# V of an attention kernel turned in blocks on VectorE instead of on TensorE and ScalarE

## Chip, core and metric

The kernel runs on one core of one Trainium2 chip. Times are device microseconds (us) of that core, from the first to the last instruction of an execution.

## What is computed

Eight sequences of 256 tokens (2048 tokens in all), model width 512. Layer norm, then causal attention with 32 query heads and 8 key/value heads of 128, rotary embedding, and scores of some keys scaled; beside it a gate network of four low-rank experts with a top-2 router. Cut to the attention and the end:

```
xn = layernorm(x)
q, k, v = xn @ wq.T, xn @ wk.T, xn @ wv.T        # heads of 128
q, k = q*cos + rotate_half(q)*sin, k*cos + rotate_half(k)*sin
scores = q @ k.T / sqrt(128) * key_scale + causal
attn = softmax(scores) @ v
out = x + (attn @ wo.T) * silu(gate_network(xn))
```

All is fp32. A product of two fp32 matrices is made of three passes on TensorE: each operand is split into a high part (fp32r, written by ScalarE: k_high, q_high, v_high, rows_high, attn_high) and a low part (the difference, by VectorE: k_low, q_low, v_low, rows_low, attn_low), and high x high, high x low and low x high are added in PSUM.

## The kernel before

**Units.** The work is cut into 32 units: 8 key/value heads by 4 blocks of 512 tokens (two sequences). A unit u has four items j of two query heads and one sequence each, n4[1] to n4[4]. Every engine has its own instruction list, written out by hand in one order: pe_unit (L629), act_unit (L936), dve_unit (L1322), and group for GpSimd (L422). Engines are tied by semaphores alone. Units 8 to 30 run in a loop, the others are unrolled; the opening, unit 0 and the closing have lists of their own (act_opening L1007, dve_opening L1399). In units 0 to 7 pieces of the gate network (pe_side, act_side, dve_side) stand between the steps.

**TensorE in unit u**, in order: turn_probs(0), output tile (1,0) of the unit before, scores(2), prob_value(0), output tile (1,1); turn_probs(1), projection of H1 for unit u+1, scores(3), prob_value(1), projection of H2, projection of V (L510 into bank_a); turn_probs(2), projection of H3, scores(0) of unit u+1, prob_value(2), projection of K for unit u+2 into bank_a (it waits for vT_done, L695), projection of H0 for u+2; turn_probs(3), output tile (0,0), scores(1) of u+1, prob_value(3), turn_v, output tile (0,1). H0 to H3 are the four query heads that share the unit's K and V. A projection is 12 matmuls of 512 columns (three_pass), an output tile too.

**V's way.** V is projected as the other kinds are, with its 128 dimensions on the partitions and the 512 tokens along them. prob_value needs it with the tokens on the partitions. So copy_vT on ScalarE (L879) moves the bank to v_T in SBUF, which also frees bank_a for K; later turn_v on TensorE (L567, four transposes of 128x128) writes it back turned into bank_a, once K's rotation has read that bank; v_high (L886) and v_low (L1264) split it from the bank into v_hi and v_lo, and prob_value(0) of the next unit waits for v_ready.

**A query head's way.** Projection, swap_halves on ScalarE (L857, L858, which move the partition halves crosswise into rot), sin_product on GpSimd (L399) beside cos_product on VectorE (L1240), rotate on VectorE (L1249, the sum of both), q_high (L865), q_low (L1255). next_scores on TensorE (L611) waits for pT_ready, that is rows_low of the item that used the same pair of banks, and for q_ready, that is q_low and k_low: scores(0) for K, H0 and H1, scores(1) for H2 and H3.

**An item's way.** scores, low_scores on ScalarE (L892), mask_rows on VectorE (L1286 to L1295), exponents (L907), row_inverse (L1305), normalise_rows (L918), turn_probs (L588), rows_high (L926) and rows_low (L1275), prob_value (L597), attn_high (L933) and attn_low (L1270), output tiles (L604), which add_tile on VectorE (L1315) adds to y_sum.

**GpSimd** also splits the weights of the next key/value head (split, L382 and L385), at fixed places of every group of four units.

## Time and profile before

| | us |
|---|---|
| median of 3 runs | 1327.3 |
| lowest and highest | 1326.88, 1327.61 |
| the profiled execution | 1326.8 |
| its span in the trace | 1324.6 |

Busy in the span: TensorE 98%, VectorE 72%, ScalarE 73%, GpSimd 32%; the granted TensorE clock is 0.999 of full. The chain that ended last lies on TensorE for 92% of the span. A timeline row gives the start, the length and the instruction; where the next row of the same engine starts before the end of this one, the two overlapped, so the distance of two starts (the step) is what an instruction costs in a row of them. The ends of matmuls are modelled.

### The profile page before, as it was taken

The numbers are of one execution on the slowest core, as the hardware profiler recorded it, in microseconds if no ns is written. First come the engines' busy times: TensorE is split into PE (matmuls) and PEld (weight loads), VectorE is DVE, ScalarE is ACT, GpSimd is POOL, SyncE is SP. The second block draws the span as 40 slices with busy tenths as digits, with TensorE's granted clock in tenths as the row PEclk, the third lists the DMA queues.
The fourth block names the chain that finished last, engine by engine and source line by source line (L and its number), as shares of the span: only waits on it lengthen the run. The fifth ranks groups of instructions, "written<-read, shape, count | busy, mean of one in ns | idle before, by whom it ended". The sixth has DMA issues, their size and how long they took to land.

```text
span 1324.6 us, 22633 instructions
## 1 busy us (share of the span) xinstructions
PE 1303.3 (98%) x7000; PEld 1106.3 (84%) x7000; DVE 953.7 (72%) x2438; ACT 972.5 (73%) x2529; POOL 427.0 (32%) x345
## 2 busy tenths in 40 slices
PE   8899999999999999999999999999999999999998
PEld 7688788888888888888888888888888888888876
DVE  7776678777777677777767777767777767777776
ACT  6877577877778777778777777777677877776874
POOL 5413312423214332233414124141431433224323
PEclk9999999999999999999999999999999999999999
DMA  6000000201101000000100001010000101002124
GB/s 230 24 1 21 25 8 9 65 28 53 40 17 32 15 25 8 16 16 16 27 5 24 8 16 32 0 32 0 24 24 0 32 8 32 8 20 95 52 82 150
DMA packets 23530, 43.66 MB, mean 33 GB/s; under 512 B 2496, under 2 KB 2752, under 8 KB 23488
## 3 DMA queue, kind: packets, MB, share of 16 engines
q1 hardware_dynamic: 20896, 38.74, 9.5%
q10 hardware_dynamic: 2592, 4.40, 0.9%
q8 instruction: 21, 0.34, 0.1%
q14 instruction: 21, 0.17, 0.0%
HBM read 34.74 MB, written 8.39 MB: 33 GB/s over the span
## 4 chain that ended last, share of the span: by engine, by line
PE 92%; ACT 3%; DVE 3%; issue 1%; DMA 0%; DVEq 0%; ACTq 0%
PE bank_b L510 19%; PE bank_a L510 18%; PE bank_b L604 13%; PE o_ps L604 12%; PE pv_ps L597 10%; PE pair L581 8%; PE pair L588 6%; PE pair L577 2%; PE pair L579 1%; PE o_ps L510 1%; PE bank_a L567 1%; ACT x_sb L1000 1%; ACT probs L918 0%; ACT probs L907 0%; ACT rot L857 0%
## 5 line engine op out<-in xcount | busy, mean ns | idle before, releaser
L399 POOL TENSOR_TENSOR rot<-rot,tab 128x512 f32<-128x512 f32 x160 | 207.1, 1296 | 593.2 <-ACT rot L858 592.9
L907 ACT ACTIVATE probs<-probs,row_min 128x128 f32<-128x128 f32 (+1 forms) x512 | 225.7, 447 | 0.2
L926 ACT ACTIVATE pT_hi<-pair 128x768 fp32r<-128x768 f32 x128 | 104.0, 812 | 164.5 <-PE pair L588 163.7
L918 ACT ACTIVATE probs<-probs,row_inv 128x128 f32<-128x128 f32 (+1 forms) x512 | 190.6, 445 | 22.5 <-DVE row_inv L1305 22.1
L1275 DVE TENSOR_TENSOR pT_lo<-pair,pT_hi 128x768 fp32r<-128x768 f32 x128 | 121.6, 950 | 86.1 <-ACT pT_hi L926 85.9
L382 POOL TENSOR_TENSOR w_hi<-raw,zero 128x512 fp32r<-128x512 f32 x74 | 85.0, 1148 | 243.4 <-PE bank_a L510 126.5
L510 PE MATMUL bank_a<-xT_hi,w_hi 128*128 (+1 forms) x376 | 149.9, 399 | 0.2 <-DVE xT_lo L1145 0.2
L510 PE MATMUL bank_b<-xT_hi,w_hi 128*128 (+1 forms) x376 | 149.8, 398 | 0.0
L510 PE MATMUL bank_b<-xT_hi,w_lo 128*128 (+1 forms) x376 | 146.8, 390 | 0.0
L510 PE MATMUL bank_a<-xT_hi,w_lo 128*128 (+1 forms) x376 | 146.8, 390 | 0.0
L510 PE MATMUL bank_a<-xT_lo,w_hi 128*128 (+1 forms) x376 | 146.3, 389 | 0.0
L510 PE MATMUL bank_b<-xT_lo,w_hi 128*128 (+1 forms) x376 | 146.3, 389 | 0.0
L1255 DVE TENSOR_TENSOR q_lo<-cosx,q_hi 128x512 fp32r<-128x512 f32 x128 | 117.2, 917 | 36.0 <-ACT q_hi L865 35.8
L581 PE MATMUL pair<-k_parts,q_hi 128*128 128x256 f32 x512 | 116.7, 309 | 0.0
L588 PEld LDWEIGHTS pair<-tab,probs 128*128 128x128 f32 x768 | 90.9, 139 | 22.7 <-ACT probs L918 6.8
L588 PE MATMUL pair<-tab,probs 128*128 128x128 f32 x768 | 104.8, 272 | 4.6 <-ACT probs L918 4.6
L1286 DVE CUSTOM_DVE_ANT_0 probs<-pair,tab 128x256 f32<-128x256 f32 x256 | 106.4, 416 | 0.0
L604 PE MATMUL o_ps<-w_hi,attn_hi 128*128 128x512 f32 x252 | 104.2, 413 | 0.3 <-DVE attn_lo L1270 0.3
L1240 DVE TENSOR_TENSOR cosx<-bank_b,tab 128x512 f32<-128x512 f32 x94 | 64.7, 689 | 52.6 <-ACT rot L858 52.0
L604 PE MATMUL bank_b<-w_hi,attn_hi 128*128 128x512 f32 x252 | 101.6, 403 | 0.0
L385 POOL TENSOR_TENSOR w_lo<-raw,w_hi 128x512 fp32r<-128x512 f32 x74 | 99.5, 1345 | 5.8
L604 PE MATMUL bank_b<-w_hi,attn_lo 128*128 128x512 f32 x252 | 98.9, 393 | 0.0
(181 smaller groups left out, 3277.3 us busy)
## 6 DMA issues: line engine op xcount, KB each, us to landing
raw<-w_seq SPq DMA_DIRECT2D x76, 256.0 KB, 2.6
gate_scratch<-b_raw ACTq DMA_DIRECT2D x16, 256.0 KB, 2.0
out<-y_sum SPq DMA_DIRECT2D x16, 256.0 KB, 2.0
x_sb<-x SPq DMA_DIRECT2D x3, 1024.0 KB, 11.2
mid<-x SPq DMA_DIRECT2D x7, 256.0 KB, 2.8
mid<-gate_scratch SPq DMA_DIRECT2D x7, 256.0 KB, 3.5
raw<-x SPq DMA_DIRECT2D x7, 256.0 KB, 2.7
raw<-gate_scratch SPq DMA_DIRECT2D x7, 256.0 KB, 2.9
```

The lines of the kernel that those rows point to most:

```text
L399: nc.gpsimd.tensor_tensor(v, v, tab[:, s:s + SEQ].unsqueeze(1).to_broadcast([P, 2, SEQ]), ALU.mult).then_inc(sin_done[kind], 1)
L510: mm = nc.tensor.matmul(dst, w(a, c), xs[:, c, bass.ds(x0, BLOCK)], start=(c == 0 and n == 0), stop=(c == DC - 1 and n == 2))
L581: mm = nc.tensor.matmul(ps[:, h, 2 * P:], a[:, head, late], k[:, k1], start=(n == 0), stop=(n == 2))
L588: mm = nc.tensor.transpose(ps[:, h, s * P:(s + 1) * P], probs[:, j % 2, h, s * P:(s + 1) * P], ident)
L597: mm = nc.tensor.matmul(dst, v[:, 2 * b + kb, :], p[:, :, c:c + (P if kb else SEQ)], start=(i == 0), stop=(i == 5))
L604: mm = nc.tensor.matmul(bank, a[:, h, rows], w[:, WO + h, :], start=(h == 0 and i == 0), stop=(h == GROUP - 1 and i == 2))
L907: a = nc.scalar.activation(s, s, ACT.Exp, bias=row_min[:, j % 2, i:i + 1], scale=-1.0, accum_out=row_sum[:, i:i + 1])
L918: a = nc.scalar.activation(s, s, ACT.Copy, scale=row_inv[:, i:i + 1])
L926: nc.scalar.activation(pT_hi[:, :, :], pair[j % 2][:, :, 0:ROWS], ACT.Copy).then_inc(pThi_done, 1)
L1255: nc.vector.tensor_tensor(q_lo[:, h, :], cosx[:, BUF[kind], :], q_hi[:, h, :].bitcast(F32), ALU.subtract)\
L1275: nc.vector.tensor_tensor(pT_lo[:, :, :], pair[j % 2][:, :, 0:ROWS], pT_hi[:, :, :].bitcast(F32), ALU.subtract).then_inc(pT_ready, 1)
L1286: return nc.vector.tensor_tensor_reduce(out=probs[:, par, h, s], in0=(probs[:, par, h, 0:P], pair[par][:, h, 2 * P:])[qt], in1=tab[:, T_MA ...
```

## The change

V's bank is turned straight into v_T. turn_v_blocks on VectorE issues eight transposes for each half: each takes 32 partitions of bank_a (32 of V's dimensions) by 4 x 32 columns (32 tokens of each of the four tiles), turns its four 32x32 blocks, and writes 32 partitions by 4 x 32 columns of v_T. Inside a half the read partitions change with every instruction, the written ones after every fourth. copy_vT and turn_v go (but for the first V, which keeps both); v_high and v_low read v_T. The K projection that follows V in bank_a waits for both halves (vturn_done) instead of the copy. The lists of ScalarE and VectorE, in the units and in the opening, are put into another order. TensorE's order is the same but for turn_v.

The opening's lists are left out below; in them the same steps stand in another order, and the transposes of the second V stand before q_low(H1) and after it.

```diff
@@ -353,7 +354,7 @@
             sp.wait_ge(q_ready[H2], UNITS)
             load_xg(TILES - 1, 2)
             sp.wait_ge(q_ready[K], UNITS)
-            sp.wait_ge(vt_ps, UNITS)
+            sp.wait_ge(v_ready, UNITS)
             load_xg(TILES - 2, 3)
             for s in range(2):
                 store_tile(TILES - 6 + s)
@@ -562,7 +563,7 @@
             three_pass(bank[:, :], lambda w, c: (w_hi, w_lo)[w][:, chunk, c * P:(c + 1) * P], x0)\
                 .then_inc(proj_done[kind], 1)
 
-        def turn_v(bank=bank_a):
+        def turn_v(bank):
             for t in range(BLOCK_TILES):
                 mm = nc.tensor.transpose(bank[:, t * P:(t + 1) * P], v_T[:, t * P:(t + 1) * P], ident)
             mm.then_inc(vt_ps, 1)
@@ -692,7 +693,7 @@
             if ahead:
                 if isinstance(u, int) and u < BLOCKS - 2:
                     pe.wait_ge(xlo_done, BLOCK_TILES * (u + 3))
-                pe.wait_ge(vT_done, c2)
+                pe.wait_ge(vturn_done, value(pe, 2 * u + 2))
                 project(K, bank_a, WK, x_2, w_2)
             pe_side(u, 2, 2)
             if ahead:
@@ -709,12 +710,6 @@
             pe.wait_ge(pT_ready, n4[4])
             pe.wait_ge(attn_ready, n4[3])
             prob_value(3)
-            if not last:
-                if ahead:
-                    bank_free(K, c3)
-                else:
-                    pe.wait_ge(vT_done, c2)
-                turn_v()
             if not last:
                 bank_free(*((H0, c3) if ahead else (H3, c2)))
             output_tile(0, 1, n4[2], n4[0] if last else None)
@@ -871,19 +866,20 @@
                 act.wait_ge(scores_done, used)
             nc.scalar.activation(k_hi, k_full[:, :], ACT.Copy).then_inc(qhi_done[K], 1)
 
-        def copy_vT(count, before_count, bank=bank_a):
+        def copy_first_vT():
+            nc.scalar.wait_ge(proj_done[V], 1)
+            nc.scalar.activation(v_T[:, :], FIRST_V, ACT.Copy).then_inc(vT_done, 1)
+
+        def first_v_high():
+            nc.scalar.wait_ge(vt_ps, 1)
+            nc.scalar.activation(v_hi[:, :, :], pv_ps[:, :].rearrange("p (k d) -> p k d", k=BLOCK_TILES),
+                                 ACT.Copy).then_inc(vhi_done, 1)
+
+        def v_high(turned, used):
             act = nc.scalar
-            act.wait_ge(proj_done[V], count)
-            if before_count is not None:
-                act.wait_ge(vt_ps, before_count)
-            nc.scalar.activation(v_T[:, :], bank[:, :], ACT.Copy).then_inc(vT_done, 1)
-
-        def v_high(count, used, bank=bank_a):
-            act = nc.scalar
-            act.wait_ge(vt_ps, count)
-            if used is not None:
-                act.wait_ge(pv_done, used)
-            nc.scalar.activation(v_hi[:, :, :], bank[:, :].rearrange("p (k d) -> p k d", k=BLOCK_TILES),
+            act.wait_ge(vturn_done, value(act, 2 * turned))
+            act.wait_ge(pv_done, used)
+            nc.scalar.activation(v_hi[:, :, :], v_T[:, :].rearrange("p (k d) -> p k d", k=BLOCK_TILES),
                                  ACT.Copy).then_inc(vhi_done, 1)
 
         def low_scores(j, done):
@@ -941,56 +937,56 @@
             rows_high(0, n4[1], None if first else n4[0])
             normalise_rows(1, n4[2])
             low_scores(2, n4[3])
+            attn_high(0, n4[1], None if first else n4[-2])
             if not last:
                 q_high(H0, c2, n4[3])
+            exponents(2, n4[3])
             rows_high(1, n4[2], n4[1])
-            attn_high(0, n4[1], None if first else n4[-2])
-            exponents(2, n4[3])
             act_side(u, 1, 0)
             if not last:
                 swap_halves(H1, bank_a, c2, H0, c2)
             low_scores(3, n4[4])
+            if not last:
+                k_high(c2, n4[4])
             act_side(u, 1, 1)
-            if not last:
-                k_high(c2, n4[4])
             normalise_rows(2, n4[3])
+            if not last:
+                swap_halves(H2, bank_b, c2, K, c2)
             attn_high(1, n4[2], None if first else n4[-2])
-            if not last:
-                swap_halves(H2, bank_b, c2, K, c2)
             act_side(u, 1, 2)
             if not last:
                 q_high(H1, c2, n4[3])
             act_side(u, 1, 3)
             rows_high(2, n4[3], n4[2])
             exponents(3, n4[4])
+            if not last:
+                swap_halves(H3, bank_b, c2, H1, c2)
             act_side(u, 2, 0)
             if not last:
-                copy_vT(c2, c1)
-                swap_halves(H3, bank_b, c2, H1, c2)
                 low_scores(0, n4[5])
+            normalise_rows(3, n4[4])
             act_side(u, 2, 1)
-            normalise_rows(3, n4[4])
+            attn_high(2, n4[3], None if first else n4[0])
             if not last:
                 q_high(H2, c2, n4[4])
-            attn_high(2, n4[3], None if first else n4[0])
             act_side(u, 2, 2)
+            if is_unit(u, 1):
+                b_high()
             if ahead:
                 swap_halves(K, bank_a, c3, H2, c2)
-            if is_unit(u, 1):
-                b_high()
             if not last:
                 q_high(H3, c2, n4[4])
             if ahead:
                 swap_halves(H0, bank_b, c3, H3, c2)
+            rows_high(3, n4[4], n4[3])
             act_side(u, 2, 3)
-            rows_high(3, n4[4], n4[3])
             if not last:
                 exponents(0, n4[5])
                 low_scores(1, n4[6])
                 normalise_rows(0, n4[5])
             attn_high(3, n4[4], None if first else n4[0])
             if not last:
-                v_high(c2, n4[4])
+                v_high(c1, n4[4])
                 exponents(1, n4[6])
 
         def x_shifted(t0, t1, count):
...
@@ -1259,9 +1254,28 @@
             nc.vector.wait_ge(qhi_done[K], count)
             nc.vector.tensor_tensor(k_lo, k_full[:, :], k_hi.bitcast(F32), ALU.subtract).then_inc(q_ready[K], 1)
 
-        def v_low(count, bank=bank_a):
+        def turn_v_blocks(count, half):
+
+
+            dve = nc.vector
+            dve.wait_ge(proj_done[V], count)
+            dve.wait_ge(v_ready, value(dve, count - 1))
+            src = bank_a[:, :].rearrange("p (t i a) -> p t i a", t=BLOCK_TILES, i=4)
+            dst = v_T[:, :].rearrange("p (t d) -> p t d", t=BLOCK_TILES)
+            for i in range(2 * half, 2 * half + 2):
+                for j in range(4):
+                    ins = nc.vector.transpose(dst[32 * i:32 * i + 32, :, 32 * j:32 * j + 32],
+                                              src[32 * j:32 * j + 32, :, i, :])
+            ins.then_inc(vturn_done, 1)
+
+        def first_v_low():
+            nc.vector.wait_ge(vhi_done, 1)
+            nc.vector.tensor_tensor(v_lo[:, :, :], pv_ps[:, :].rearrange("p (k d) -> p k d", k=BLOCK_TILES),
+                                    v_hi[:, :, :].bitcast(F32), ALU.subtract).then_inc(v_ready, 1)
+
+        def v_low(count):
             nc.vector.wait_ge(vhi_done, count)
-            nc.vector.tensor_tensor(v_lo[:, :, :], bank[:, :].rearrange("p (k d) -> p k d", k=BLOCK_TILES),
+            nc.vector.tensor_tensor(v_lo[:, :, :], v_T[:, :].rearrange("p (k d) -> p k d", k=BLOCK_TILES),
                                     v_hi[:, :, :].bitcast(F32), ALU.subtract).then_inc(v_ready, 1)
 
         def attn_low(j, done):
@@ -1337,153 +1351,160 @@
             mask_rows(2, n4[3])
             if not last:
                 q_low(H0, c2)
+            attn_low(0, n4[1])
             if not first:
                 tile_in(1, 1)
+            row_inverse(n4[3])
             rows_low(1, n4[2])
-            attn_low(0, n4[1])
             dve_side(u, 1, 0)
-            row_inverse(n4[3])
             if not last:
                 cos_product(H1, bank_a, c2, H0, c2)
             mask_rows(3, n4[4])
             dve_side(u, 1, 1)
             if not last:
+                k_low(c2)
                 rotate(H1, c2)
-                k_low(c2)
                 cos_product(H2, bank_b, c2)
+            attn_low(1, n4[2])
             dve_side(u, 1, 2)
+            if not last:
+                turn_v_blocks(c2, 0)
+            rows_low(2, n4[3])
             if not last:
                 q_low(H1, c2)
             dve_side(u, 1, 3)
-            rows_low(2, n4[3])
-            attn_low(1, n4[2])
-            if not last:
-                rotate(H2, c2)
             if is_unit(u, 1):
                 split_ar()
-            if is_unit(u, 2):
-                split_b()
+            if not last:
+                turn_v_blocks(c2, 1)
             row_inverse(n4[4])
+            if not last:
+                cos_product(H3, bank_b, c2, H1, c2)
             dve_side(u, 2, 0)
             if not last:
-                cos_product(H3, bank_b, c2, H1, c2)
                 mask_rows(0, n4[5])
             dve_side(u, 2, 1)
             if not last:
+                rotate(H2, c2)
                 rotate(H3, c2)
+            attn_low(2, n4[3])
+            if not last:
+                q_low(H2, c2)
             dve_side(u, 2, 2)
-            if not last:
-                q_low(H2, c2)
-                q_low(H3, c2)
             if ahead:
                 cos_product(K, bank_a, c3, H2, c2)
+            if not last:
+                q_low(H3, c2)
             rows_low(3, n4[4])
-            attn_low(2, n4[3])
-            tile_in(0, 0)
             if ahead:
                 cos_product(H0, bank_b, c3, H3, c2)
             dve_side(u, 2, 3)
+            tile_in(0, 0)
             if not last:
                 row_inverse(n4[5])
                 mask_rows(1, n4[6])
             if ahead:
                 rotate(K, c3)
             attn_low(3, n4[4])
-            tile_in(0, 1)
             if ahead:
                 rotate(H0, c3)
             if not last:
                 v_low(c2)
                 row_inverse(n4[6])
+            if is_unit(u, 2):
+                split_b()
+            tile_in(0, 1)
...
```

## Rows read from the trace of the kernel before

**Rows 1.** The page's part 1: busy us (share of the span) and instructions.

```profile
PE 1303.3 (98%) x7000; PEld 1106.3 (84%) x7000; DVE 953.7 (72%) x2438; ACT 972.5 (73%) x2529; POOL 427.0 (32%) x345
```

**Rows 2.** Table of stretches: stretch, its us, busy us (instructions) by engine, clock, DMA.

```profile
45.00:81.00 36.00, 32.00 (x172) 26.53 (x171) 26.48 (x72) 32.88 (x76) 13.88 (x12) 0.95 0.09 23
...
640.00:960.00 320.00, 320.00 (x1723) 273.42 (x1721) 230.77 (x587) 236.56 (x622) 103.43 (x83) 1.00 0.06 17
```

**Rows 3.** TensorE's waits, 321 to 1283 us, longest: us, times, longest one.

```profile
PE pair L588 <- ACT probs L918: 1.2, 1, 1.2
```

**Rows 4.** Chain that ended last, one unit: start us, us, what.

```profile
602.36 2.72 PE bank_a L510 x12
...
610.71 2.72 PE bank_a L510 x12
...
621.80 0.44 PE bank_a L567 x4
622.24 2.77 PE bank_b L604 x12
...
650.10 2.72 PE bank_a L510 x12
```

**Rows 5.** Timeline of ScalarE: start us, us long, engine, line, what, count.

```profile
602.39 0.60 ACT L857 ACTIVATE rot<-bank_b 64x512 f32<-64x512 f32 x1 [0.63 <-PE bank_b L510]
603.00 0.59 ACT L858 ACTIVATE rot<-bank_b 64x512 f32<-64x512 f32 x1
603.62 0.63 ACT L865 ACTIVATE q_hi<-cosx 128x512 fp32r<-128x512 f32 x1
605.77 0.81 ACT L926 ACTIVATE pT_hi<-pair 128x768 fp32r<-128x768 f32 x1 [1.52 <-PE pair L588]
...
608.24 0.58 ACT L879 ACTIVATE v_T<-bank_a 128x512 f32<-128x512 f32 x1
```

**Rows 6.** Timeline of VectorE in the same unit.

```profile
601.03 0.29 DVE L1286 CUSTOM_DVE_ANT_0 probs<-probs,tab 128x128 f32<-128x128 f32 x1
...
601.24 0.29 DVE L1286 CUSTOM_DVE_ANT_0 probs<-probs,tab 128x128 f32<-128x128 f32 x1
...
603.62 0.69 DVE L1240 TENSOR_TENSOR cosx<-bank_b,tab 128x512 f32<-128x512 f32 x1 [0.88 <-ACT rot L858]
604.28 1.24 DVE L1255 TENSOR_TENSOR q_lo<-cosx,q_hi 128x512 fp32r<-128x512 f32 x1
606.62 0.96 DVE L1275 TENSOR_TENSOR pT_lo<-pair,pT_hi 128x768 fp32r<-128x768 f32 x1 [1.10 <-ACT pT_hi L926]
607.49 0.68 DVE L1270 TENSOR_TENSOR attn_lo<-pv_ps,attn_hi 128x512 fp32r<-128x512 f32 x1
608.09 0.68 DVE L1249 TENSOR_TENSOR cosx<-cosx,rot 128x512 f32<-128x512 f32 x1
...
625.21 0.69 DVE L1315 TENSOR_TENSOR y_sum<-bank_b,y_sum 128x512 f32 x1 [0.94 <-PE bank_b L604]
```

**Rows 7.** Timeline of VectorE around gm_T, which writes from partition 64 on.

```profile
205.35 0.69 DVE L1178 TENSOR_TENSOR gm_T<-o_ps,gm_T 64x512 fp32r<-64x512 f32 x1
206.06 0.69 DVE L1240 TENSOR_TENSOR cosx<-bank_b,tab 128x512 f32<-128x512 f32 x1
206.67 0.41 DVE L1292 TENSOR_TENSOR probs<-pair,probs 128x256 f32<-128x256 f32 x1
```

**Rows 8.** Timeline of TensorE, same unit: first matmul of scores(0), then of K.

```profile
608.32 0.28 PE L577 MATMUL pair<-k_parts,q_hi 128*128 128x256 f32 x1
...
610.55 0.39 PE L510 MATMUL bank_a<-xT_hi,w_hi 128*128 x1
```

**Rows 9.** Timeline of GpSimd: same unit, then a unit with weight splits.

```profile
603.67 1.30 POOL L399 TENSOR_TENSOR rot<-rot,tab 128x512 f32<-128x512 f32 x1 [3.33 <-ACT rot L858]
...
723.08 1.48 POOL L382 TENSOR_TENSOR w_hi<-raw,zero 128x512 fp32r<-128x512 f32 x1
...
727.03 1.62 POOL L385 TENSOR_TENSOR w_lo<-raw,w_hi 128x512 fp32r<-128x512 f32 x1
```

More of the change, by code:

```diff
@@ L1447, in dve_opening @@
[L1447 to L1453 removed]
+            mask_rows(2, 3)
+            rows_low(1, 2)
+            attn_low(0, 1)
+            q_low(H0, 2)
+            dve_side(0, 1, 0)
+            rotate(K, 2)
+            cos_product(H1, bank_a, 2, H0, 2)
+            shifts(12, 16, 7)
+            attn_low(1, 2)
+            dve_side(0, 1, 1)
```

123 lines of the change are left out of this document (58 added, 65 removed).

## The prediction

> **What bounds the kernel now.** I read the busy shares first [rows 1]. TensorE is busy for 1303.3 of 1324.6 us and VectorE, the next of interest, for 72%. The table of stretches [rows 2] says where TensorE is not: 32.00 of 36 us in the opening stretch, but 320.00 of 320 us in the middle, while VectorE works 230.77 us there. Then TensorE's own waits [rows 3]: between 321 and 1283 us the longest that it spent for anybody is 1.2 us in one place. So in the middle its issue order is the time: a matmul that goes away is worth its full price, and a wait that is new costs its full length, since TensorE has no later gap to lose it in. Last, the chain that ended last, over one unit [rows 4]: the K projection begins at 610.71 and again at 650.10 us, so a unit takes 39.39 us.
>
> **What is removed.** Four turnings of V on TensorE: 0.44 us in the chain [rows 4]. Each matmul is 0.27 us long in the record, but they overlap, so the chain's piece is the price. The first V stays on TensorE, 31 units lose it: 31 x 0.44 = 13.6 us. On ScalarE the copy of V, 0.58 us [rows 5], also goes. ScalarE is busy 73% [rows 1] and TensorE hardly waits for it [rows 3], so I count that at zero. What hides it is the gap in front of its next swap or rows_high; if that gap were gone, the copy would be worth up to 0.5 us a unit.
>
> **What is added: the price of one block transpose.** No row of before shows one. Its data are 128 elements a lane. From below: two masked minima of 128 elements follow each other at 601.03 and 601.24, so a step of 0.21 us although each lasts 0.29 [rows 6]; the engine overlaps an instruction with the end of the one before. I see no reason for anything below that step. From above: that overlap has an exception in this trace. The one instruction that writes from partition 64 on, gm_T, starts at 205.35 and lasts 0.69; its successor starts at 206.06, which is 0.71 later, where the next step after it, of the same length, is 0.61 (206.06 to 206.67) [rows 7]. ScalarE does the same: its two half copies, which move between partition halves, follow at 0.61 us for a length of 0.60 (602.39, 603.00, 603.62) [rows 5]. In the change each of the 16 transposes reads other partitions than the one before it. I take it that each waits for the end of its predecessor: 0.29 + 0.02 = 0.31 us. If each 4-byte element also needed two passes, the row of 256 elements, 0.41 us long (the last of [rows 7]), would be the nearest: 0.43 us. Ends 0.21 and 0.43; I take 0.31, as gm_T is the row that shares the trait. So 16 x 0.31 = 4.96 us more on VectorE a unit, on 28.4 us of 39.39 (230.77 / 320 x 39.39) [rows 2]: there is room on average, so the order decides.
>
> The Trainium skill, page "VectorE: DVE Perf Modes", section "Two Vector instructions with no wait between them", has a rule that speaks against this change: an instruction is held until all earlier ones are finished if its input or its output starts in another group of 32 partitions than the last. For the output gm_T agrees; for the input alone no run here shows it, and that is what all sixteen hang on. The same page, section "The three transpose paths", gives 311 ns for a VectorE transpose of 128 columns of blocks, and its table of rules sends a full turning to TensorE; 16 x 0.311 is an estimate of 4.98 us by that page, and no row here has the operation.
>
> **Where it lies.** V's projection (L510 into bank_a) ends at 602.36 + 2.72 = 605.08 [rows 4]. TensorE then issues turn_probs(2), the H3 projection, and at 608.32 the first matmul of scores(0) [rows 8]: 3.24 us after V. The K projection of the unit after next, which overwrites V's bank and waits for vturn_done, follows at 610.55 [rows 8]: 5.47 us after V. VectorE sees a TensorE end 0.20 us late (output tile ends 622.24 + 2.77 = 625.01, y_sum starts 625.21) [rows 4, 6]. The new order of VectorE is then: half of the turning, rows_low(2), q_low(H1), the other half. rows_low(2) steps 0.87 (606.62 to 607.49) and could begin 1.54 us after V; q_low(H1) has 512 elements a lane, so 0.69 us (the cosx at 603.62) with a step of 0.60 (607.49 to 608.09) [rows 6]; a release to another engine costs 0.04 (pT_hi ends 606.58, pT_lo starts 606.62) [rows 5, 6]. scores(0) waits for rows_low(2) and for q_low(H1). Before the change q_low(H1) stood ahead of rows_low(2) and was long done.
> - scores(0): 0.20 + 8 x 0.31 + 0.87 + 0.69 + 0.04 = 4.28 us after V, where 3.24 is wanted: 1.04 us late.
> - K projection: 0.20 + 2.48 + 0.87 + 0.60 + 2.48 + 0.04 = 6.67, where 5.47 is wanted: 1.20 us late. The first delay is within this one, they don't add.
> VectorE is free when V ends at 605.08: cos_product(H2) runs from 603.62 to 604.28 [rows 6], and in the new order only attn_low(1), a step of 0.60, lies between it and the turning, so to 604.88. Behind the waiting turning stand rows_low(2), q_low(H1), row_inverse and cos_product(H3); the last two have 3 us or more.
>
> **The sum.** 23 units (8 to 30) have no side work: 22 x 1.20 + 1.04 (unit 30 has no K projection to hold up) = 27.4. In units 0 to 7 side pieces of the gate network stand between V and K on TensorE and give cover, while their VectorE parts take some: I count half, 8 x 0.60 = 4.8. And q_low(H1), which has both inputs in SBUF, can't run beside a GpSimd instruction: at 604.28 it took 1.24 instead of 0.68 (608.09, both inputs in SBUF too) while one ran from 603.67 to 604.97 [rows 6, 9]. That cost nothing where it stood; in its new place, some 3.5 us after V, GpSimd splits weights in two of four units (in the one with V's end at 723.22 without a gap from 723.08 to 728.65, the first and the last of four in [rows 9]), so 0.55 x 12 = 6.6. The 13.6 us go off: 27.4 + 4.8 + 6.6 - 13.6 = +25.2. The opening's lists are reordered too; its 4 idle us of 36 [rows 2] bound that at some 3 us either way, I take 0. v_high and v_low now read v_T in SBUF; should GpSimd stretch v_low by 0.55, TensorE still has the output tile of 2.77 us [rows 4] and another behind it before prob_value(0) asks for V, so nothing; without that cover it would be the 0.55. SP now waits for the last v_ready instead of vt_ps, ahead of one pair of loads that the closing uses a unit later: nothing, or some of one load's time if that slack were gone. 1326.8 (the profiled execution; its span is 1324.6, with 2.2 us around it, and the median of the three runs is 0.5 higher) + 25.2 = 1352.0.
>
> **Rivals.**
> 1. The transposes overlap like other instructions (0.21). Speaks for: the masked minima; against: gm_T and the half copies. scores(0): 0.20 + 1.68 + 0.87 + 0.69 + 0.04 = 3.48, 0.24 late; K: 0.20 + 1.68 + 1.47 + 1.68 + 0.04 = 5.07, in time. 23 x 0.24 + 8 x 0.12 = 6.5 lost, 13.6 won: 1319.7, up to 1326 with GpSimd's full share. I say 1321: this is the other sign. It turns where the delay a unit equals 0.44: q_low(H1) ready 3.68 us after V, so a transpose at 0.235 us.
> 2. All is covered: transposes at 0.18 or less, or VectorE sees V earlier than I read. 1326.8 - 13.6 = 1313.2.
> 3. Two passes an element (0.43): K: 0.20 + 3.44 + 1.47 + 3.44 + 0.04 = 8.59, 3.12 late; 22 x 3.12 + 2.0 + 8 x 1.56 - 13.6 + 6.6 = +76.1: 1403.
>
> **How the numbers follow.** Forecast 0.52, rival 1 0.28, rival 2 0.10, rival 3 0.10. The forecast's own range: at 0.29 a transpose K is 0.88 late, which gives with no share of GpSimd 1337; at 0.35 it is 1.84 late, with twice that share 1375. The whole range reaches down to rival 1's better end and leaves out 2 and 3: 1316 to 1376. A measurement of this kernel tells about 0.2% (2.7 us) from no change. Faster: rival 2 and most of rival 1, 0.35; same: 0.07; slower: 0.58.
>
> **What would show it.** Right: TensorE's first matmul of scores(0) or of bank_a's K projection waits for VectorE in nearly every unit, 1.0 to 1.3 us in all; the transposes start 0.31 us apart, each after the end of the last; a unit of some 40.2 us between two K projections. Wrong: a step of 0.2 us and no such waits (rival 1 or 2), or a new wait elsewhere, on rows_low(3) or attn_low, because VectorE is 5 us a unit fuller; or q_low(H1) done before the turning's end.

## The result, and the profile after

The changed kernel takes 1391.06 us (median of four runs, 1387.42 to 1392.47) against 1327.40 us: a ratio of 1.0479, interval 1.0466 to 1.0492. The change costs 64 us where I had forecast 25, and the time lies above the range too. The profiled execution took 1391.42 us, its span is 1389.2.

The page's part 1 of the changed kernel answers to [rows 1], the two lines behind it are the page's part 4 (the share of each engine in the chain that ended last) and a group of its part 5 (line, engine, operation, count | busy us, mean ns | idle before):

```profile
PE 1312.3 (94%) x6876; PEld 1098.2 (79%) x6876; DVE 1098.0 (79%) x2934; ACT 964.6 (69%) x2498; POOL 424.0 (31%) x345
...
PE 77%; DVE 17%; issue 4%; ACT 2%; DMA 0%; POOL 0%; DVEq 0%; ACTq 0%; POOLq 0%
...
L1267 DVE STREAM_TRANSPOSE v_T<-bank_a 32x128 f32<-32x128 f32 x496 | 155.0, 312 | 16.3 <-PE bank_a L511 9.2
```

124 matmuls are gone, as forecast, and 496 block transposes of 312 ns are there. VectorE is at 79% only, but it now holds 17% of the chain. TensorE has idle time in the middle, which it had not [rows 2]. The table of stretches says so from 45 us to the start of unit 8's prob_value(0), from there to unit 30's, and for the window of rows 2 (stretch, its us, busy us by engine, clock, DMA):

```profile
45.00:411.50 366.50, 346.37 (x1806) 288.51 (x1807) 287.98 (x782) 260.29 (x665) 99.95 (x80) 0.98 0.08 26
411.50:1322.30 910.80, 870.65 (x4578) 730.80 (x4577) 728.89 (x1943) 636.64 (x1672) 282.11 (x224) 1.00 0.07 21
...
640.00:960.00 320.00, 306.75 (x1614) 258.14 (x1614) 254.09 (x680) 224.91 (x592) 98.25 (x78) 0.99 0.06 16
```

TensorE's waits from 330 to 1340 us (us, times, longest) name who is late. In [rows 3] the longest was 1.2 us, once:

```profile
PE pair L578 <- DVE q_lo L1250: 33.2, 24, 1.9
PE bank_a L511 <- DVE v_T L1267: 7.2, 20, 0.4
```

L578 is the first matmul of scores(0), bank_a L511 that of the K projection. One loop unit of VectorE, whose V projection ends at 633.27 (timeline; it answers to [rows 6]):

```profile
632.44 0.69 DVE L1284 TENSOR_TENSOR attn_lo<-pv_ps,attn_hi 128x512 fp32r<-128x512 f32 x1
633.40 2.58 DVE L1267 STREAM_TRANSPOSE v_T<-bank_a 32x128 f32<-32x128 f32 x8 [0.27 <-PE bank_a L511]
636.01 0.96 DVE L1289 TENSOR_TENSOR pT_lo<-pair,pT_hi 128x768 fp32r<-128x768 f32 x1
636.88 0.68 DVE L1250 TENSOR_TENSOR q_lo<-cosx,q_hi 128x512 fp32r<-128x512 f32 x1
637.60 2.61 DVE L1267 STREAM_TRANSPOSE v_T<-bank_a 32x128 f32<-32x128 f32 x8
```

And TensorE in the same unit (it answers to [rows 8]):

```profile
632.88 0.39 PE L511 MATMUL bank_a<-xT_hi,w_lo 128*128 x1
...
637.71 0.36 PE L578 MATMUL pair<-k_parts,q_hi 128*128 128x256 f32 x1 [1.04 <-DVE q_lo L1250]
...
640.54 0.49 PE L511 MATMUL bank_a<-xT_hi,w_hi 128*128 x1 [0.37 <-DVE v_T L1267]
```

This is the forecast's picture step by step: the turning starts 0.13 us after V, both waits are on the queue behind it, scores(0) begins 4.44 us after V's end (before 3.24) and K 7.27 us after it (before 5.47). From the start of one unit's prob_value(0) to the next it is 40.82 us, against 39.38, and in every second unit 41.69: there q_low(H1) lasts 1.54 us, while GpSimd splits weights.

Measured as the start of each unit's prob_value(0) against the same of before, the lateness (called delay below) grows like this: 18.3 us by unit 8, 61.8 by unit 30 (1.98 a unit), 64.6 at the end.

### The profile page after: what moved, and what is told of

It reads as the page before. It is cut to its first block, busy times and chain, and to the rows that moved or that the text cites. A ratio compares the mean times of both kernels' runs of the same rounds, so it can differ in the third digit from the quotient of the medians.

```text
span 1389.2 us, 22925 instructions
## 1 busy us (share of the span) xinstructions
PE 1312.3 (94%) x6876; PEld 1098.2 (79%) x6876; DVE 1098.0 (79%) x2934; ACT 964.6 (69%) x2498; POOL 424.0 (31%) x345
## 4 chain that ended last, share of the span: by engine, by line
PE 77%; DVE 17%; issue 4%; ACT 2%; DMA 0%; POOL 0%; DVEq 0%; ACTq 0%; POOLq 0%
PE bank_a L511 19%; PE bank_b L511 12%; PE bank_b L605 12%; PE o_ps L605 11%; DVE v_T L1267 9%; PE pv_ps L598 8%; PE pair L582 6%; PE pair L589 4%; DVE pT_lo L1289 2%; DVE q_lo L1250 2%; PE pair L578 2%; PE o_ps L511 1%; PE pair L580 1%; ACT rot L853 0%; DVE cosx L1235 0%
## 5 line engine op out<-in xcount | busy, mean ns | idle before, releaser
L1267 DVE STREAM_TRANSPOSE v_T<-bank_a 32x128 f32<-32x128 f32 x496 | 155.0, 312 | 16.3 <-PE bank_a L511 9.2
L511 PE MATMUL bank_a<-xT_hi,w_hi 128*128 (+1 forms) x376 | 154.6, 411 | 9.8 <-DVE v_T L1267 7.2
L383 POOL TENSOR_TENSOR w_hi<-raw,zero 128x512 fp32r<-128x512 f32 x74 | 82.2, 1111 | 252.0 <-PE bank_a L511 137.7
L511 PE MATMUL bank_b<-xT_hi,w_hi 128*128 (+1 forms) x376 | 150.0, 399 | 0.0
L511 PE MATMUL bank_a<-xT_hi,w_lo 128*128 (+1 forms) x376 | 148.4, 395 | 0.0
L511 PE MATMUL bank_a<-xT_lo,w_hi 128*128 (+1 forms) x376 | 147.9, 393 | 0.0
L511 PE MATMUL bank_b<-xT_hi,w_lo 128*128 (+1 forms) x376 | 146.8, 390 | 0.0
L511 PE MATMUL bank_b<-xT_lo,w_hi 128*128 (+1 forms) x376 | 146.5, 390 | 0.0
L888 ACT ACTIVATE probs<-pair 128x256 f32<-128x256 f32 x128 | 49.3, 385 | 131.1 <-PE pair L582 130.2
L578 PE MATMUL pair<-k_parts,q_hi 128*128 128x256 f32 x256 | 75.8, 296 | 46.2 <-DVE q_lo L1250 42.2
L582 PE MATMUL pair<-k_parts,q_hi 128*128 128x256 f32 x512 | 117.2, 311 | 0.0
L1250 DVE TENSOR_TENSOR q_lo<-cosx,q_hi 128x512 fp32r<-128x512 f32 x128 | 113.6, 890 | 0.4 <-ACT q_hi L860 0.3
L860 ACT ACTIVATE q_hi<-cosx 128x512 fp32r<-128x512 f32 x128 | 80.3, 629 | 35.1 <-DVE cosx L1244 34.4
```

Of the source, the lines that this page charges most:

```text
L511: mm = nc.tensor.matmul(dst, w(a, c), xs[:, c, bass.ds(x0, BLOCK)], start=(c == 0 and n == 0), stop=(c == DC - 1 and n == 2))
L582: mm = nc.tensor.matmul(ps[:, h, 2 * P:], a[:, head, late], k[:, k1], start=(n == 0), stop=(n == 2))
L1250: nc.vector.tensor_tensor(q_lo[:, h, :], cosx[:, BUF[kind], :], q_hi[:, h, :].bitcast(F32), ALU.subtract)\
L1267: ins = nc.vector.transpose(dst[32 * i:32 * i + 32, :, 32 * j:32 * j + 32], src[32 * j:32 * j + 32, :, i, :])
```

## Experiments

All edits are to the changed kernel unless another is named. "Delay" is always the start of a unit's prob_value(0) against before's.

### q_low(H1) back ahead of the turning

```diff
             if not last:
+                q_low(H1, c2)
                 turn_v_blocks(c2, 0)
             rows_low(2, n4[3])
-            if not last:
-                q_low(H1, c2)
```

> In the loop the step q_low(H1) of VectorE goes back ahead of the first eight transposes; nothing else changes. Theory A (the time is lost in the serial VectorE work between the end of V's projection and K's, and q_low(H1) in the middle of it costs 0.72 us in every unit and another 0.85 us in every second one, where it meets a weight split on GpSimd): the odd and even units become alike, the first matmul of scores(0) comes 4.1 us after V's end instead of 4.4 and 5.3, that of K 6.8 us instead of 7.3 and 8.1, a unit takes 40.4 us, the kernel some 1364. Rival B (VectorE as a whole is too full, so that the order of its steps matters little): the unit stays within 0.3 us of 41.3 and the kernel within 10 us of 1391.

Measured: 1367.31 us, ratio to before 1.0304 (1.0274 to 1.0334). TensorE's waits, 330 to 1270 us:

```profile
PE pair L578 <- DVE pT_lo L1289: 14.1, 25, 0.7
PE bank_a L511 <- DVE v_T L1267: 8.9, 21, 0.5
```

Now every unit takes 40.47 us, with scores(0) 4.00 and K 6.92 us after V: rows_low(2) is the late one instead of q_low(H1), and the alternation of 40.82 and 41.69 is gone, since q_low(H1) no longer meets the weight splits. So the order of VectorE's list is worth 24 us of the 64; 1364 us was expected. The other 40 stay with the transposes in their place.

### Two copies in place of sixteen transposes

V isn't turned in this kernel.

```diff
-            for i in range(2 * half, 2 * half + 2):
-                for j in range(4):
-                    ins = nc.vector.transpose(...)
-            ins.then_inc(vturn_done, 1)
+            s = slice(256 * half, 256 * half + 256)
+            nc.vector.tensor_copy(v_T[:, s], bank_a[:, s]).then_inc(vturn_done, 1)
```

> The sixteen transposes are left out: two plain VectorE copies of 128 x 256 take their place, so V is not turned and the output isn't attention's. All else, the new lists of ScalarE and VectorE too, is as after. Theory A (the transposes' own length is the whole loss, the reordered lists are sound): no wait of TensorE in the loop but under 0.3 us at scores(0), a unit of 38.95 to 39.2 us, the kernel 1313 to 1322. Rival C (the reordered lists lose time by themselves, above all in the opening and the units with side work, which came out 18 us later by the end of V's eighth projection): the loop's unit falls to 39.0 but the first eight units keep 8 us or more of their loss, the kernel 1325 or more.

Measured: 1318.60 us, ratio 0.9932 (0.991 to 0.9955). The lists, the waits and all that the change removes are the same as in the changed kernel; only 16 times 0.32 us became 2 times 0.42. So the rearranged lists cost nothing worth naming: at unit 8 the kernel is 5.5 us ahead of the kernel before. Some 8 to 9 of the 13.6 us that I had counted as gain are there once VectorE is quick. Not all: in one unit of four scores(0) waits 0.5 us for q_low(H1), more than the 0.3 that I had expected at most, and such a unit takes 39.70 us where the best take 39.00. It is the length of the turning that costs.

### The same partitions in a run of four

Each group of four transposes reads one set of 32 partitions and writes one set; the blocks land in the wrong place.

```diff
-                                              src[32 * j:32 * j + 32, :, i, :])
+                                              src[32 * i:32 * i + 32, :, j, :])
```

> The same sixteen transposes, but four in a row now read and write one and the same group of 32 partitions, so only every fourth begins on new partitions; what they write is not V turned. Theory A (a transpose waits for the end of its predecessor only because its partitions change): inside a four the starts are 0.20 to 0.22 us apart, across fours 0.32; eight take 1.9 us instead of 2.6; K comes some 5.9 us after V's end, the kernel 1335 to 1350. Rival D (a block transpose always runs alone, whatever its partitions): the starts stay 0.32 us apart and the kernel at 1391.

Measured: 1334.03 us, ratio 1.0056 (1.0033 to 1.0078). The chain that ended last (start, us, what) and the timeline of VectorE for the first eight of a unit:

```profile
607.90 0.90 DVE v_T L1267 x4
608.80 0.01 issue
608.81 0.54 DVE v_T L1267 x3
609.35 0.11 issue
609.46 0.27 DVE v_T L1267
```
```profile
607.90 1.82 DVE L1267 STREAM_TRANSPOSE v_T<-bank_a 32x128 f32<-32x128 f32 x8 [0.27 <-PE bank_a L511]
```

Two of the eight by themselves:

```profile
608.14 0.26 DVE L1267 STREAM_TRANSPOSE v_T<-bank_a 32x128 f32<-32x128 f32 x1
608.34 0.26 DVE L1267 STREAM_TRANSPOSE v_T<-bank_a 32x128 f32<-32x128 f32 x1
```

In the changed kernel each transpose is a piece of its own in the chain, and the next starts 0.01 us or little more after its end. Here they overlap, so a step is read from the starts: 0.65 us for three (608.81 to 609.46). One by one it is 0.24 us behind the first of a four, 0.20 behind the second and third (608.14 to 608.34), and 0.28 where the partitions change, while each lasts 0.27 (the median by tile; 0.311 in the changed kernel). So the change of partitions takes the overlap away, and the instructions last 0.04 us longer as well. Eight take 1.82 instead of 2.58 us. The same data, the same form and the same count: it is the change of partitions that makes 0.32 out of 0.20 to 0.24, and 57 of the 64 us hang on it. That it was two passes an element (my rival 3) or a dear instruction in itself falls.

Even so nothing is won. From the first start to rows_low(2) eight take 1.86 us, 0.23 each, which is where the prediction put the turn (0.235). scores(0) still begins 3.69 us after V, 0.45 late, and most units take 39.41 us against 39.38.

### Only the written partitions change

The reads stay in one group of 32 partitions, and each transpose writes another group than the one before it.

```diff
-            for i in range(2 * half, 2 * half + 2):
-                for j in range(4):
+            for j in range(4):
+                for i in range(2 * half, 2 * half + 2):
                     ins = nc.vector.transpose(...,
-                                              src[32 * j:32 * j + 32, :, i, :])
+                                              src[64 * half:64 * half + 32, :, j, :])
```

> As after, but all eight transposes of a half read one group of 32 partitions, while the written group alternates with each; what they write is not V turned. In after, three of four neighbours change only the group that is read, and start 0.32 us apart. If a change of the written group alone holds an instruction too, the starts stay 0.32 us apart here and the time near 1391; if only the read group counts, they fall to 0.21 us and the kernel to some 1335.

Measured: 1381.38 us, in a single run, so this time has no interval. The chain has its first transposes at

```profile
629.69 0.30 DVE v_T L1267
630.00 0.01 issue
630.01 0.31 DVE v_T L1267
630.32 0.01 issue
630.33 0.30 DVE v_T L1267
```

0.32 us apart, as in the changed kernel, where three of four neighbours change only the read group. So either side alone holds the next instruction. (The 10 us less than in the changed kernel lie elsewhere: 4.5 of them in the first eight units, and in the loop one unit in four is a long one of 41.6 us, where there it is one in two.) The sixteen transposes have sixteen different pairs of read and written group, so in whatever order they follow each other, one side changes each time. The Trainium skill, page "VectorE: DVE Perf Modes", section "Two Vector instructions with no wait between them", states this rule for input and output; the runs agree with both halves, 0.32 us held and 0.20 to 0.24 us not.

### Four and twelve instead of eight and eight

```diff
-                turn_v_blocks(c2, 0)
-            rows_low(2, n4[3])
-            if not last:
                 q_low(H1, c2)
+                turn_v_part(c2, 0, 4)
+            rows_low(2, n4[3])
...
-                turn_v_blocks(c2, 1)
+                turn_v_part(c2, 4, 16)
```

turn_v_part(count, first, end) does the transposes first to end of the sixteen.

> As the kernel with q_low(H1) ahead, but split four and twelve around rows_low(2) instead of eight and eight. Theory A (the two waits of TensorE nest; only the one at K, the end of all sixteen, sets the unit): the wait at scores(0) goes away (first matmul at 3.2 us after V's end), K stays at some 6.8 us, the unit at 40.4 us and the kernel within 4 us of the kernel with q_low(H1) ahead. Rival E (each wait of TensorE costs by itself, as restarting it does): the kernel gains another 0.3 us a unit, 8 us or more.

Measured: 1370.62 us, ratio 1.0329 (1.0299 to 1.0359). scores(0) begins 3.24 us after V, as before the change, and K still 6.91 us after it. TensorE's waits, 330 to 1270 us:

```profile
PE bank_a L511 <- DVE v_T L1280: 27.5, 22, 1.3
```

The wait of scores(0) is gone and K's is as much longer, so a unit takes 40.5 us as in the first experiment. The two waits nest: only the end of the turning counts, and the other split gains nothing as long as K stands where it does. The kernel's time is 3.3 us above that of the first experiment, with intervals that overlap.

### K after H0

TensorE projects H0 ahead of K, and the lists of the other engines follow (H0 and H3 ahead of K and H2); the transposes are split 4, 6 and 6. TensorE's part of the edit:

```diff
-                pe.wait_ge(vturn_done, value(pe, 2 * u + 2))
-                project(K, bank_a, WK, x_2, w_2)
-            pe_side(u, 2, 2)
-            if ahead:
                 bank_free(H3, c2)
                 project(H0, bank_b, WQ, x_2, w_2)
+            pe_side(u, 2, 2)
+            if ahead:
+                pe.wait_ge(vturn_done, value(pe, 2 * u + 2))
+                project(K, bank_a, WK, x_2, w_2)
```

> V's turning is the same sixteen transposes with the same partitions, but TensorE projects H0 (into the other bank) before K, so the bank of V is wanted 2.7 us later; VectorE's order is q_low(H1), four transposes, rows_low(2), six, cos_product(H3), six, and ScalarE and GpSimd take H0 and H3 before K and H2. Theory A (the loss is a deadline that is 1.4 us too short, not VectorE's load): K's first matmul is wanted 8.2 us after V's end and v_T is ready at 7.7, so no wait there; H0's needs cos_product(H3) at 5.4 us and may wait 0.1 us; a unit of 38.95 to 39.2 us, the kernel 1313 to 1322, faster than before. Rival B (VectorE is too full: 33 of 39 us with chains through ScalarE in it): the wait only moves to scores(1), which wants rows_low(3) and two q_low, or to turn_probs(3); the unit stays over 39.9 us and the kernel over 1345.

Measured: 1356.87 us, ratio 1.0224 (1.0207 to 1.0241). I had expected 1313 to 1322; the time lies with the rival. The turning is covered in the loop: the delay is 20.9 us at unit 8 and 26.5 at unit 30, 0.25 a unit. Two things that I had not seen come out. The wait moved: scores(1) now waits for rows_low(3) in seven units, because two q_low stand ahead of it beside GpSimd's work. TensorE's wait, and VectorE's timeline in such a unit:

```profile
PE pair L580 <- DVE pT_lo L1304: 5.5, 7, 1.8
```
```profile
638.30 2.82 DVE L1251 TENSOR_TENSOR q_lo<-cosx,q_hi 128x512 fp32r<-128x512 f32 x2
641.05 0.68 DVE L1236 TENSOR_TENSOR cosx<-bank_b,tab 128x512 f32<-128x512 f32 x1
641.65 0.94 DVE L1304 TENSOR_TENSOR pT_lo<-pair,pT_hi 128x768 fp32r<-128x768 f32 x1
```

And 20.9 of the 30.5 us that are lost by the end are lost in the first eight units, which I had priced at next to nothing.

### The low parts first

On top of that, mask_rows(0) stands behind both q_low, and rows_high(3) ahead of K's swap. The edit against the last experiment:

```diff
+            rows_high(3, n4[4], n4[3])
             if ahead:
                 swap_halves(K, bank_a, c3, H2, c2)
-            rows_high(3, n4[4], n4[3])
...
                 rotate(H2, c2)
-                mask_rows(0, n4[5])
...
                 q_low(H2, c2)
+                mask_rows(0, n4[5])
```

> The kernel with K after H0, where two things are moved: VectorE makes q_low(H3) and q_low(H2) ahead of mask_rows(0), before GpSimd's next product begins, and ScalarE makes rows_high(3) ahead of K's swap. Its loop still lost 0.25 us a unit against before, at scores(1), where two q_low took 2.8 us beside GpSimd. Theory A (every single wait that is left has a place and a cover): the wait at scores(1) falls under 0.2 us, the loop's unit from 39.65 to 39.0 to 39.2 us, the kernel to 1341 to 1348, the rest being the first eight units with side work. Rival B (VectorE is too full for any order): the unit stays at 39.5 us or more and the kernel at 1353 or more.

Measured: 1352.68 us, ratio 1.018 (1.0165 to 1.0196), above the expected 1341 to 1348. In the loop 0.11 us a unit are left (17.7 at unit 8, 20.1 at unit 30). The first eight units keep their 17.7.

### The old way in units 0 to 7

Units 0 to 7 and the opening turn V on TensorE as in the kernel before, with its lists; the loop is as in the last experiment. TensorE's part of the edit, against the kernel before:

```diff
+        def is_old(u):
+            return isinstance(u, int) and u < WRITTEN
...
-                pe.wait_ge(vT_done, c2)
-                project(K, bank_a, WK, x_2, w_2)
+                if is_old(u):
+                    pe.wait_ge(vT_done, c2)
+                    project(K, bank_a, WK, x_2, w_2)
+                else:
+                    bank_free(H3, c2)
+                    project(H0, bank_b, WQ, x_2, w_2)
```

> Units 0 to 7, the opening too, are those of the kernel before (V turned on TensorE, old lists); from unit 8 on the kernel with q_low ahead of mask_rows and K after H0. Theory A: the first eight units, which cost the other kernels 15 to 21 us because their side work leaves no room on VectorE for 5 us more, come out as before, and the rest gains 0.2 to 0.4 us a unit over 23 units: 1317 to 1323, faster than before. Rival B (the loss in the first eight units was the opening's new order or a shift that the loop would have taken anyway): 1330 or more.

Measured: 1334.16 us, ratio 1.0047 (1.0033 to 1.0061); expected were 1317 to 1323, a miss. The delay is -0.3 us at unit 8, 2.2 at unit 30 and 7.6 at unit 31. So the first eight units' loss arises in these units. It isn't the opening's new order: in the changed kernel prob_value(0) of unit 0 still starts 0.4 us early. What in these units costs is read from the trace in the next section. The 5.4 us behind unit 30, which has no K and no H0 projection as cover, are a wait of 2.76 us for rows_low and TensorE at half rate afterwards (granted clock 0.54 from 1294 to 1298 us). And in the loop the expected 0.44 us a unit is missing even in units where the list of waits shows none. The chain that ended last, in such a unit:

```profile
570.51 1.06 PE pv_ps L615 x6
571.57 0.13 issue
571.70 2.99 PE bank_b L525 x12
```

The H0 projection waits 0.13 us for its bank, which cos_product(H3) on VectorE frees, and is then 2.99 us long in the chain instead of 2.72 [rows 4]: 0.40 together, the price of what was saved. Part of the 0.27 is the way a chain is cut: without a stop a projection's first matmul starts 0.16 us before the last one ahead of it ends (610.55 and 610.71 in the kernel before), and the chain counts it from that end. From its first start on it is 2.99 against 2.88 us, so it starts 0.29 us late and is 0.11 us longer.

### K behind the turning of the probabilities

On top of the last: output tile, H0, turn_probs(3), K in this order, and the last turning (in unit 30) again on TensorE. ScalarE's and VectorE's lists in the loop are rearranged with it, the transposes split 4 and 12. TensorE's part of the edit:

```diff
+                output_tile(0, 0, n4[2], n4[-1], weights=w_0, uses=0)
+                bank_free(H3, c2)
+                project(H0, bank_b, WQ, x_2, w_2)
+                pe.wait_ge(probs_ready, n4[4])
+                turn_probs(3)
+                pe.wait_ge(vturn_done, value(pe, 2 * u - 14))
+                project(K, bank_a, WK, x_2, w_2)
```

> V on VectorE from unit 8 to 29 alone, sixteen transposes as they are; unit 30, which has no K and H0 to project and so 5.4 us less cover, is as before too. In the loop TensorE takes output tile (0,0) ahead of H0 and K behind turn_probs(3): V's bank is wanted 11.6 us after V's end and H3's 8.2 us, where v_T is ready at 6.6 and cos_product(H3) at 7.2. Theory A (the whole loss was deadlines, and 5.2 us more of VectorE fit in a unit once nothing waits for them): no wait of TensorE over 0.1 us in a unit, a unit of 38.95 to 39.05 us against 39.38 before, the kernel 1316 to 1320, faster than before by 0.6%. Rival B (with VectorE at 84% its in-order list keeps one late step somewhere, which eats the 0.44 us as it did in the kernel whose loop alone was new): unit 39.3 us or more, kernel 1325 or more.

Measured: 1331.70 us, ratio 1.0031 (1.0018 to 1.0043), where 1316 to 1320 was expected. The loss behind unit 30 is gone. H0 doesn't wait, and two units of four take 38.92 us, so there the whole 0.44 is won. In the other two (40.1 and 40.3 us) the next output tile waits:

```profile
PE o_ps L622 <- DVE attn_lo L1370: 7.9, 12, 0.9
```

K's cos_product, which waits 0.79 us for ScalarE's swap (at 620.57 us), and mask_rows(1) now stand directly ahead of attn_low(3) on VectorE. What the one wait lost, another took.

### One head of the output tile ahead of H0

The lists of ScalarE and VectorE go back to those of the kernel with the old way in units 0 to 7, but for rows_low(3), which stands ahead of H0's cos_product. TensorE's part, against the last experiment:

```diff
-                output_tile(0, 0, n4[2], n4[-1], weights=w_0, uses=0)
+                pe.wait_ge(attn_ready, n4[2])
+                pe.wait_ge(y_added, n4[-1])
+                pe.wait_ge(w_ready[CHUNKS - 1], w_0)
+                output_heads(0, 0, o_ps[:, :], range(0, 1))
                 bank_free(H3, c2)
                 project(H0, bank_b, WQ, x_2, w_2)
-                pe.wait_ge(probs_ready, n4[4])
-                turn_probs(3)
                 pe.wait_ge(vturn_done, value(pe, 2 * u - 14))
                 project(K, bank_a, WK, x_2, w_2)
+                pe.wait_ge(probs_ready, n4[4])
+                turn_probs(3)
+                output_heads(0, 0, o_ps[:, :], range(1, GROUP)).then_inc(o_done, 1)
```

> The kernel whose loop alone is new (K after H0), where its quiet units lose all of their 0.44 us at one place: H0's first matmul comes 0.13 us late for cos_product(H3), and its projection takes 2.99 us instead of 2.72. Here TensorE takes the first head (three matmuls, 0.69 us) of output tile (0,0) ahead of H0 and the other three behind turn_probs(3), VectorE takes rows_low(3) ahead of cos_product(H0), and unit 30 is as before. Theory A (a wait of any length costs its length and 0.27 us more for the restart of the weight loads): the wait and the 0.27 go, quiet units 38.95 us, the kernel 1317 to 1321, faster than before by 0.5 to 0.8%. Rival F (the longer projection has another cause, for instance the bank's other user): H0's projection stays at 2.99 us and the kernel at 1325 or more.

Measured: 1327.78 us, ratio 1.0009 (1.0000 to 1.0018): level with the kernel before, where 1317 to 1321 was expected. The chain that ended last, where the kernel with the old way in units 0 to 7 had the wait:

```profile
570.98 1.05 PE pv_ps L615 x6
572.03 0.68 PE o_ps L622 x3
572.71 2.72 PE bank_b L525 x12
```

Without the wait the projection is 2.72 us again in the chain. So the longer projection goes with the stop, and my theory on this point held. Two units of four take 39.0 us, 0.37 less than before the change. The other two take 39.7 and 39.8, where output tile (1,0) still waits for attn_low(3), 4.4 us in all, 12 times: the gain of the one half pays for the other.

### attn_low(3) ahead of rotate(K)

```diff
+            attn_low(3, n4[4])
             if ahead:
                 rotate(K, c3)
-            attn_low(3, n4[4])
```

> The kernel with one head ahead, and rotate(K) moved behind attn_low(3) on VectorE in the loop. Its wait that was left, 4.4 us in 12 places, is output tile (1,0)'s for attn_low(3), up to 0.4 us each. Theory A: those waits go with their restarts, 0.3 to 0.67 us in every second unit, and none takes their place: 3 to 6 us less, 1321 to 1325. Rival B (in a VectorE list that is 84% full the lateness only goes to the next step, here v_low or rows_low(0)): 1326 or more.

Measured: 1327.55 us, ratio 1.0006 (0.9997 to 1.0015): no gain, as the rival had it. TensorE's waits, 330 to 1270 us:

```profile
PE pair L595 <- DVE pT_lo L1392: 4.3, 12, 1.0
```

The 4.4 us for attn_low are now 4.3 us for rows_low, again twelve times. No version of the turning on VectorE beat the kernel before.

## Why the prediction was wrong

**What held.** TensorE without slack; both waits at their places and nested; q_low(H1) as the last link to scores(0); the stretching by GpSimd in every second unit; and the choice of 0.31 us for a transpose that waits for its predecessor, against 0.21 and 0.43. gm_T was the right neighbour, though it could not tell input from output. Rival 1 (they overlap) fell with the chain of the changed kernel, rival 2 with the waits, rival 3 with the same-partition run. Rival 1's step of 0.21 was well chosen for a transpose that isn't held (0.20 to 0.24), but the sixteen are held.

**The sum, by its terms.** Forecast +25.2, measured 64.6 in the profiled executions.

1. *The first eight units: forecast 4.8 - 8 x 0.44 = +1.3, measured +18.3.* This is the step that failed most. I took the side work as half a cover (8 x 0.60 late). It covers on TensorE, but its VectorE part stands ahead of the turning, and I never read one such unit. Unit 3, VectorE's timeline; V ends at 206.88:

```profile
206.65 0.21 DVE L1217 TENSOR_TENSOR gate<-gate,keep 128x64 f32<-128x64 f32 x1
...
207.91 1.43 DVE L1225 TENSOR_TENSOR mid<-mid,gate 128x256 f32<-128x256 f32 x4
209.26 2.58 DVE L1267 STREAM_TRANSPOSE v_T<-bank_a 32x128 f32<-32x128 f32 x8
211.87 0.96 DVE L1289 TENSOR_TENSOR pT_lo<-pair,pT_hi 128x768 fp32r<-128x768 f32 x1
212.74 0.68 DVE L1250 TENSOR_TENSOR q_lo<-cosx,q_hi 128x512 fp32r<-128x512 f32 x1
213.45 2.61 DVE L1267 STREAM_TRANSPOSE v_T<-bank_a 32x128 f32<-32x128 f32 x8
```

   The turning starts 2.38 us after V instead of 0.13, scores(0) 6.69 us after V (before 4.68), K 10.88 (before 7.02). TensorE's wait, and the table of stretches behind it:

```profile
213.57 0.55 PE L578 MATMUL pair<-k_parts,q_hi 128*128 128x256 f32 x1 [2.83 <-DVE q_lo L1250]
```
```profile
214.00:218.00 4.00, 4.00 (x17) 3.71 (x17) 3.79 (x11) 1.76 (x5) 0.00 (x0) 0.50 0.00 0
```

   K doesn't wait here: the turning ends at 216.06 and K starts at 217.76. Of its 3.86 us, 2.01 are scores(0)'s lateness; the other 1.85 come from the granted clock, which is at 0.50, the level of 1.2 GHz, after the wait. The K projection, in the chain, begins at that pace too:

```profile
217.96 3.74 PE bank_a L511 x12
```

   From 45 us to unit 8's prob_value(0) TensorE is idle for 366.50 - 346.37 = 20.1 us; before the change it was 5.8 (342.45 busy of 348.20 us). Its two largest waits there:

```profile
PE pair L578 <- DVE q_lo L1250: 7.8, 7, 2.8
PE o_ps L553 <- DVE b_raw L1177: 5.1, 3, 1.7
```

   The second is the side work itself: in units 4 to 6 the gate network's matmuls ahead of K wait for its own VectorE step (L1177), which stands behind the second half of the turning. So this cover on TensorE was a waiter for VectorE too. The clock adds to it: at the half level TensorE is busy for 15.6 us here, before for 3.4, and half of the difference is 6.1 us (an estimate). 14.4 more idle, 6.1 for the clock and 3.5 won (8 x 0.44) make 17.0 of the 18.3. The run with the old way in units 0 to 7 agrees: with these units and the opening put back, the delay at unit 8 goes from 17.7 to -0.3.

2. *The delay of K in a loop unit: forecast 1.20, measured 1.80.* Against the working of 6.67 us: the two halves take 2.61 each from start to successor, not 2.48 (a step of 0.326, not 0.31), +0.26. q_low(H1) steps 0.72, not 0.60, since the transpose behind it is held too, +0.12. From the end of the last transpose to TensorE it is 0.33 us, where I had 0.04 from a release between ScalarE and VectorE, +0.29. VectorE sees V's end after 0.13, not 0.20, -0.07. Together 7.27. Another 0.13 comes behind it: after the stop the K projection is longer (3.01 us from its first matmul on, before 2.88). The run with q_low(H1) ahead has the same terms: the turning starts 0.38 us after V, as q_low(H1) and the hold behind it end there, then 2.61, 0.99 for rows_low(2) with a held successor, 2.61 and 0.33: 6.92, and a unit is 0.35 us shorter than the 40.82.

3. *GpSimd: forecast 0.55 in every second unit, measured 0.86 (41.69 against 40.82).* Right in kind; the row that I took the price from [rows 6] met only the end of a GpSimd instruction. With q_low(H1) moved away the alternation is gone.

4. *The clock, not forecast.* In two loop units TensorE's granted clock fell after a wait of 1.90 us at scores(0); in the other nine with the same wait it stayed. The table of stretches and the chain behind the V projection that ends at 674.11, where a unit takes 42.6 us:

```profile
682.00:686.00 4.00, 4.00 (x14) 3.09 (x13) 3.97 (x15) 2.61 (x6) 0.00 (x0) 0.73 0.15 53
```
```profile
682.49 0.63 PE L511 MATMUL bank_a<-xT_hi,w_hi 128*128 x1
...
684.18 0.40 PE L511 MATMUL bank_a<-xT_lo,w_hi 128*128 x1
```

   A matmul of the projection is 0.63 us long and 0.43 from the next at the level of 1.2 GHz, then 0.40 and 0.23 again at 2.4 GHz. It costs some 0.9 us each time.

The loop is thus 43.5 us (22 units) against 23.3, 20.2 more: 2.9 from GpSimd, 1.8 from the clock, and the remaining 15.5 from the delay and the longer projection (22 x 0.73 would be 16.1). The 0.6 that I had for unit 30 are 2.8; there the granted clock is 0.50 from 1346.33 to 1349.75, some 1.7 us by the same estimate. Forecast +25.2, and +17.0, +20.2 and +2.2 more, makes 64.6.

**The range.** Its upper end came from 0.35 us a transpose and a double share of GpSimd. The release (0.04) and the side units (half a cover) had one value each and no upper bound, and the clock had none at all; they hold most of the miss.

**What stays open.** Why a release after a transpose takes 0.33 us where one after q_low(H1) takes 0.15. Why the projection behind a short stop is 0.11 to 0.13 us longer. Why the clock fell after some waits of 1.90 us and not after others. Whether a turning of another shape would do: with sixteen pieces of 32 by 128 no order escapes the hold, and other pieces weren't tried.

## What to carry to other kernels

Where the first engine has no slack, a cheap step there (0.44 us) isn't moved to another engine by its busy share, but by the length of the chain up to the next thing that waits: here 16 x 0.32 us in a gap of 5.5 us that already held two other steps. A wait on the first engine can also cost it its clock afterwards, and in unit 3 that more than doubled the price. Read one unit of every kind, also those with side work, in the second engine's order before calling side work a cover. A wait that is removed on a full path turns up at the next latest input; the kernel is only faster if the whole list behind it becomes shorter.

## What the runs showed that I had not expected

- A 32x128 fp32 block transpose steps 0.20 to 0.24 us when its neighbour uses the same partitions, and 0.32 in a row where the read or the written group changes each time, on an instruction of 0.27 to 0.31 us.
- A stop of TensorE of 0.13 us by the chain cost 0.40 us: the projection behind it starts 0.29 us late and is 0.11 longer. In the kernel with one head ahead, whose order leaves the stop out, both are gone.
- In unit 3 a wait of 2.83 us was followed by half the clock, which cost 1.85 us before K and 1.0 in it, more than the 2.01 us that scores(0) was late.
- From the last transpose to the waiting matmul it is 0.33 us, from q_low(H1) 0.15.
- q_low(H1), 0.68 us long alone, took 1.54 us beside a weight split, 0.86 more; two of them took 2.82.
